# Graph layers on one core: where the inverse of the distance root is made for the third layer's first three units

## The chip, the cores and the metric

The kernel runs on one core of one Trainium2 chip. The metric is the device time of one execution in microseconds (us). The five instruction queues that matter here are PE (TensorE, the matmuls, with its weight loads shown apart as PEld), DVE (VectorE), ACT (ScalarE), POOL (GpSimd) and SP (SyncE, which issues loads). Each works through its own list in order and waits on semaphores that the others raise.

## The reference, cut to what matters

Four graph layers work on 4096 nodes of 64 features, x (4096 x 64), with one adjacency matrix adj (4096 x 4096). Each layer takes the layer norm of x, clips it below at zero, and adds its own result to x. The third (`L2_gnn`) is a layer in hyperbolic space. Cut to its core it is

```python
h = jnp.maximum(_layernorm(x, axis=-1), 0.0)          # 4096 x 64
deg = jnp.maximum(adj.sum(axis=1, keepdims=True), 1e-08)
w = adj / deg
log_ij = _logmap(h[:, None, :], h[None, :, :], c)      # c = 1, all pairs of nodes
agg = jnp.einsum('ij,ijc->ic', w, log_ij)
x = x + _expmap(0, agg @ weight + bias, c)

def _logmap(x, y, c):
    sub = _mobius_add(-x, y, c)
    sub_norm = norm(sub)
    arg = jnp.clip(sub_norm, 0.0, TANH_CLIP)
    return 2.0 / lam_x * jnp.arctanh(arg) * sub / sub_norm
```

For each pair of nodes the kernel needs one scalar out of this, arctanh(norm)/norm up to factors of the nodes. It gets it from a number z of the pair (a product of node rows): the root r = sqrt(z^2 - 1), the logarithm tau = ln(z + r), and the factor tau / r. The pair factor times the adjacency entry is then the weight with which a node's row enters the sum.

## The kernel before, in words

**Layers and units.** Layers run one after the other. The third layer walks the 4096 x 4096 square of pairs in 72 units (`UNITS`, lines 67 to 71), numbered n = 0 to 71. A unit is 256 nodes by 512, held as one tile of 128 partitions x 1024 columns (128x1024, f32). The pair factor is symmetric, so most units also serve the mirrored block: PE transposes them, and a second product with the adjacency entries (far) follows. Units 0 and 1 are not mirrored; unit 2 is the first that is. Units 0 to 2 are all full tiles.

**The work of one unit n**, by engine, with lines of the kernel before:
- PE `scores2(n)`: z of the unit into two PSUM banks of four matmuls (L859) and some small bf16 ones (L582). From n = 2 on it waits for `sum_ready` n - 1, the sum of unit n - 2, since there are two z buffers (`ROT` = 2).
- ACT `square2(n)`: z squared (L1243), raises `square_ready`.
- PE `sides2(n)`: small bf16 matmuls into the same banks (L582), raises `side_ready`.
- DVE `rest2(n)`: z^2 - 1, floored (L1977), raises `rest_ready`.
- ACT `roots2(n)`: the logarithm of that (L1249) into `lnr`; the exponential of half of it, which is the root, into `sums(n)` (L1257), raises `root_ready`; the exponential of minus half of it, which is the root's inverse, over the logarithm in `lnr` (L1260), raises `rin_ready`.
- DVE `sum2(n)`: waits for `root_ready` and `side_ready`, adds z and the root in place (L1983), raises `sum_ready`.
- ACT `arc2(n)`: the logarithm of the sum (L1264), raises `tau_ready`.
- DVE `pair2(n)`: waits for `tau_ready` and `rin_ready`, the product of the two (L1989), raises `pair_ready`.
- POOL: pair factor times adjacency (L560, near). PE `mirror2(n)`: eight transposes (L891), and DVE `far2(n)` multiplies them by the adjacency (L1996). Then PE gathers both (L582).

**Order.** The order on every engine is written out by hand. ACT runs, for each n: `roots2(n)`, extra steps, `square2(n + 1)`, `arc2(n)` (for n = 0 the square of unit 1 stands inside `roots2(0)`). DVE runs, for each n: copies of finished strips, `sum2(n)`, `far2(n - 1)` if mirrored, `rest2(n + 1)`, extra steps (`second_half2`, `last_passage2`), `pair2(n)`. PE runs, for each n: `scores2(n + 1)`, `sides2(n)`, `mirror2(n - 1)`, the gathers of unit n - 2. The extra steps are what is left of the second layer for its second half of the nodes, and pieces of the fourth: on DVE a copy of 128x1024 at n = 0 and at n = 2 (L1469, `second_half2`), and from n = 3 on rows of small operations.

**Buffers.** `lnr` and `root` have two slots, `sums` three. `roots2(n)` waits for `pair_ready` n - 1, the pair of unit n - 2, before it writes `lnr`. Loads of the adjacency for the units go through five slots that come free with the gathers.

Of the kernel before, what the change touches and what calls it, by code (L numbers as in the profile page):

```python
# [17 lines left out]
ACT = mybir.ActivationFunctionType  # L18
# [34 lines left out]
ROT = 2  # L53
# [18 lines left out]
HALVED = (4, 5, 6, 7)  # L72
FLIPS = (16, 18)
AUX_R, AUX_L = 13, 14


GROUPS = ((0, 8), (8, 16), (16, 32))
# [29 lines left out]
def mirrored(n):  # L107
    S, p = UNITS[n]
    return p >= 2 * S + 2 or S in HALVED and p == 2 * S
# [8 lines left out]
def first_col(n):  # L118

    S, p = UNITS[n]  # L120
    return PAIR if S in HALVED and p == 2 * S + 1 else 0


def mirrors(n):

    return sum(mirrored(m) for m in range(n + 1))
# [24 lines left out]
def graph_layers(nc, x, adj_t, codes, w0_t, b0, w1_t, b1, wq_t, bq, wk_t, bk, scalars, w2, b2, w3, b3, out):  # L151
    ctx = ExitStack()
    with ctx:
# [5 lines left out]
        def sem(name):  # L159
            if name not in named:  # L160
                named[name] = ctx.enter_context(nc.semaphore(name))
            return named[name]
# [78 lines left out]
        def units_of(first, n):  # L241
            return work[:, first * UNIT:(first + n) * UNIT].rearrange("p (k n) -> p k n", k=n)
        root, lnr = units_of(0, ROT), units_of(2, ROT)

        def sums(n):
            k = (4, 16, 17)[n % ROTS]
            return work[:, k * UNIT:(k + 1) * UNIT]
# [27 lines left out]
        def z_banks(n):  # L275
            return banks(4 + 2 * (n % ROT), 6 + 2 * (n % ROT))

        def live(ap, n):

            c = first_col(n)  # L280
            return ap.rearrange("p (q n) -> p q n", q=2)[:, :, c:] if c else ap
# [782 lines left out]
        def _(act):  # L1064
# [176 lines left out]
            def square2(n):  # L1241
                act.wait_ge(sem("z_ready"), n + 1)
                nc.scalar.activation(live(root[:, n % ROT, :], n), live(z_banks(n), n), ACT.Square).then_inc(sem("square_ready"), 1)  # L1243

            def roots2(n):
                act.wait_ge(sem("rest_ready"), n + 1)
                if n >= ROT:
                    act.wait_ge(sem("pair_ready"), n - ROT + 1)
                nc.scalar.activation(live(lnr[:, n % ROT, :], n), live(root[:, n % ROT, :], n), ACT.Ln).then_inc(sem("lnr_ready"), 1)  # L1249
                act.wait_ge(sem("lnr_ready"), n + 1)  # L1250
                if 0 < n < ROTS:
                    act.wait_ge(sem("agg1_done"), 4 * T - 2 + n)
                if n >= ROTS:
                    act.wait_ge(sem("near_ready"), n - ROTS + 1)
                    if mirrored(n - ROTS):
                        act.wait_ge(sem("mirror_ready"), mirrors(n - ROTS))
                nc.scalar.activation(live(sums(n), n), live(lnr[:, n % ROT, :], n), ACT.Exp, scale=0.5).then_inc(sem("root_ready"), 1)  # L1257
                if n == 0:
                    square2(1)
                nc.scalar.activation(live(lnr[:, n % ROT, :], n), live(lnr[:, n % ROT, :], n), ACT.Exp, scale=-0.5).then_inc(sem("rin_ready"), 1)  # L1260

            def arc2(n):
                act.wait_ge(sem("sum_ready"), n + 1)
# [70 lines left out]
            for n in range(NU):  # L1334
                roots2(n)
                last_passage2(n)
                second_half2(n)
                if 1 < n + 1 < NU:
                    square2(n + 1)
                arc2(n)  # L1340
# [56 lines left out]
        def _(dve):  # L1397
            V = nc.vector
# [580 lines left out]

            def sum2(n):  # L1980
                dve.wait_ge(sem("root_ready"), n + 1)
                dve.wait_ge(sem("side_ready"), n + 1)
                V.scalar_tensor_tensor(live(sums(n), n), live(z_banks(n), n), 1.0, live(sums(n), n), ALU.max, ALU.add)\  # L1983
                 .then_inc(sem("sum_ready"), 1)
# [36 lines left out]
            for n in range(NU):  # L2021
                if n >= 3 and mirrored(n - 3):
                    far2_out(n - 3)
                if n >= 3 and closes(n - 3) and n - 3 not in EARLY:
                    near2_out(n - 3)
                sum2(n)
                if n >= 1 and mirrored(n - 1):
                    far2(n - 1)
                if n + 1 < NU:
                    rest2(n + 1)  # L2030
                second_half2(n)
                last_passage2(n)
                if n - 2 in EARLY:
                    near2_out(n - 2)
                if n == NU - 1:
                    power(0)
                pair2(n)

            n = NU - 1
# [96 lines left out]
```

## Time and profile before

| what | value |
|---|---|
| median of 3 runs | 1099.08 us (1094.03 to 1100.4) |
| the profiled execution's own time | 1094.24 us |
| its span, from first instruction to last | 1092.5 us |
| busy share PE / DVE / ACT / POOL | 95% / 79% / 70% / 25% |
| mean granted TensorE clock | 0.989 |
| third layer's units | from 553.5 us to about 980 us |

The profile shows one execution. Busy time is the time in which an engine had an instruction in work; on an engine, the next instruction may start some 0.1 us before the one ahead of it ends. The chain of waits goes back from the last instruction to what released it, and "issue" in it is time for which the profile names no cause. A row of the timeline gives the start, the duration, and in brackets how long the engine sat idle before it and for whom.

### The profile page before, as it was taken

To read this page: it belongs to the slowest core of one execution; us is meant where nothing else is said; L and a number is where in the kernel's file an instruction comes from. 1 tells how busy PE (TensorE), PEld (TensorE's weight loads), DVE (VectorE), ACT (ScalarE), POOL (GpSimd) and SP (SyncE) were. 2 spreads that over 40 slices of the span, in tenths; PEclk is the share of its full clock that TensorE was granted. 3 is DMA by queue.
4 is the path that set the end of the run, shared out by engine and by line. 5 is a ranking of instruction groups with operands and counts; after the bars stand their busy time and mean duration, and the time that the engine had idled before them with its cause. 6 is when DMAs were issued, how large, how long until landed. Compare 5 with 4: busy or idle time off the path is not lost.

```text
span 1092.5 us, 14983 instructions
## 1 busy us (share of the span) xinstructions
PE 1035.0 (95%) x5462; PEld 451.6 (41%) x5462; DVE 859.5 (79%) x1021; ACT 760.0 (70%) x807; POOL 267.9 (25%) x146
## 2 busy tenths in 40 slices
PE   7999999999689999999979988999999998989998
PEld 2333333337633333334324443444544554436544
DVE  7999989996766666697669977887789887887781
ACT  4555455553556666686698989988888888886682
POOL 1089400000010000004015364434433433330010
PEclk9999999999989999999999999999999999999999
DMA  9999989980048888787754345555555546446441
GB/s 347 398 349 424 384 317 357 357 324 28 1 158 272 286 284 282 252 276 270 250 174 154 118 133 174 186 165 188 163 171 168 186 142 193 148 154 214 141 174 39
DMA packets 98453, 240.42 MB, mean 220 GB/s; under 512 B 16464, under 2 KB 47184, under 8 KB 82000
## 3 DMA queue, kind: packets, MB, share of 16 engines
q1 hardware_dynamic: 89168, 222.72, 60.1%
q10 hardware_dynamic: 9216, 16.78, 4.0%
q8 instruction: 43, 0.70, 0.2%
q14 instruction: 26, 0.21, 0.1%
HBM read 221.65 MB, written 17.83 MB: 219 GB/s over the span
## 4 chain that ended last, share of the span: by engine, by line
PE 53%; issue 21%; POOL 13%; DVE 7%; ACT 4%; DMA 1%; POOLq 0%; SPq 0%; DVEq 0%; ACTq 0%
PE PS L582 38%; POOL ring L560 10%; PE PS L756 5%; PE PS L757 5%; POOL H L560 2%; PE PS L594 1%; ACT work L1180 1%; DVE work L1989 1%; PE PS L616 1%; DMA X<-in_x 1%; PE PS L891 1%; DVE work L1621 1%; DVE ring L1996 0%; PE PS L907 0%; ACT work L1387 0%
## 5 line engine op out<-in xcount | busy, mean ns | idle before, releaser
L1662 DVE TENSOR_TENSOR work<-work,ring 128x1024 f32<-128x1024 f32 x128 | 151.2, 1223 | 76.6 <-ACT work L1180 76.5
L1180 ACT ACTIVATE work<-PS,att_sc 128x1024 f32<-128x1024 f32 x128 | 147.6, 1201 | 85.7 <-PE PS L757 78.4
L1115 ACT ACTIVATE work<-PS 128x1024 uint8<-128x1024 f32 x128 | 124.0, 1020 | 107.6 <-PE PS L582 107.6
L560 POOL TENSOR_TENSOR ring<-work,ring 128x1024 f32<-128x1024 f32 (+1 forms) x57 | 134.1, 2354 | 243.2 <-DVE work L1989 243.1
L582 PE MATMUL PS<-ring,work 128*65 128x256 f32 (+1 forms) x612 | 191.2, 460 | 2.4 <-DVE work L2017 1.5
L582 PE MATMUL PS<-work 128*64 128x512 f32 (+3 forms) x800 | 153.4, 523 | 1.1 <-ACT work L1243 1.0
L1983 DVE SCALAR_TENSOR_TENSOR work<-PS,work 128x1024 f32<-128x1024 f32 x72 | 85.9, 1193 | 55.0 <-PE PS L582 47.7
L582 PEld LDWEIGHTS PS<-ring,work 128*65 128x65 f32 x612 | 82.4, 138 | 89.7 <-issue 64.7
L756 PE MATMUL PS<-work 128*128 128x512 f16 x256 | 98.9, 386 | 2.0 <-DVE work L1469 1.3
L1249 ACT ACTIVATE work<-work 128x1024 f32<-128x1024 f32 x72 | 74.3, 1031 | 36.3 <-DVE work L1977 36.3
L757 PE MATMUL PS<-work 128*128 128x512 f16 x256 | 98.1, 383 | 0.0
L1989 DVE SCALAR_TENSOR_TENSOR work<-work 128x1024 f32<-128x1024 f32 x72 | 85.7, 1190 | 2.4 <-ACT work L1264 2.0
L582 PEld LDWEIGHTS PS<-work 128*64 128x64 f32 (+2 forms) x800 | 38.2, 119 | 118.5 <-issue 110.9
L1264 ACT ACTIVATE work<-work 128x1024 f32<-128x1024 f32 x72 | 74.2, 1030 | 12.4 <-DVE work L1983 10.2
L859 PE MATMUL PS<-TB,TA 64*128 64x512 f32 (+1 forms) x288 | 79.6, 629 | 2.9 <-DVE work L1983 2.9
L891 PE MATMUL PS<-ident,work 128*128 128x128 f32 x464 | 64.6, 282 | 18.3 <-DVE work L1989 17.1
L582 PE MATMUL PS<-work,TB 128*64 128x512 bf16 x672 | 76.4, 384 | 2.1 <-DVE work L1972 2.1
L1257 ACT ACTIVATE work<-work 128x1024 f32<-128x1024 f32 x72 | 74.4, 1033 | 2.3
L582 PE MATMUL PS<-work,tri_above 128*128 128x512 bf16 x256 | 75.8, 379 | 0.0
L1243 ACT ACTIVATE work<-PS 128x1024 f32<-128x1024 f32 x72 | 70.9, 985 | 5.2 <-PE PS L582 5.1
L582 PE MATMUL PS<-work,tri_rest 128*128 128x512 bf16 x248 | 74.4, 382 | 0.0
L1525 DVE TENSOR_TENSOR TB<-TB,work 128x2048 f32<-128x2048 f32 x32 | 73.4, 2293 | 0.1
(267 smaller groups left out, 1482.9 us busy)
## 6 DMA issues: line engine op xcount, KB each, us to landing
ring<-in_adj_t SPq DMA_DIRECT2D x96, 1024.0 KB, 5.7
ring<-in_adj_t SPq DMA_DIRECT2D x107, 512.0 KB, 4.0
work<-in_adj_t SPq DMA_DIRECT2D x32, 1024.0 KB, 8.4
codes<-work ACTq DMA_DIRECT2D x64, 256.0 KB, 7.3
ring<-codes SPq DMA_DIRECT2D x64, 256.0 KB, 4.0
H<-in_adj_t SPq DMA_DIRECT2D x25, 512.0 KB, 4.2
X<-in_x SPq DMA_DIRECT2D x2, 256.0 KB, 4.8
X<-in_x SPq DMA_DIRECT2D x1, 512.0 KB, 10.1
```

Of the source, the lines that this page charges most:

```text
L560: nc.gpsimd.tensor_tensor(live(near(n), n), live(sums(n), n), live(near(n), n), ALU.mult).then_inc(sem("near_ready"), 1)
L582: return mm(out_ap, lhsT, rhs, start=starts, stop=True, skip_group_check=True)
L756: mm(o, k_hl[:, jt * P:(jt + 1) * P], q_hh[:, i0:i0 + BANK], start=True, stop=False)
L757: ins = mm(o, k_hl[:, jt * P:(jt + 1) * P], q_ll[:, i0:i0 + BANK], start=False, stop=True)
L859: mm(z_banks(n)[:, q * BANK + c:(q + 1) * BANK], TA[half_rows(q), p * P:(p + 1) * P], TB[half_rows(q), S * STRIP + c:(S + 1) * STRIP], sta ...
L891: ins = nc.tensor.transpose(PS[:, c:c + P], sums(n)[:, q * BANK + i * P:q * BANK + (i + 1) * P], ident[:, :])
L1115: nc.scalar.activation(made[:, k, u * UNIT:(u + 1) * UNIT], PS[:, (4 + 2 * u) * BANK:(6 + 2 * u) * BANK], ACT.Relu).then_inc(sem("codes_ma ...
L1180: nc.scalar.activation(att[:, u, :], PS[:, (4 + 2 * u) * BANK:(6 + 2 * u) * BANK], ACT.Sigmoid, bias=att_sc[:, 2:3], scale=att_sc[:, 1:2]) ...
L1257: nc.scalar.activation(live(sums(n), n), live(lnr[:, n % ROT, :], n), ACT.Exp, scale=0.5).then_inc(sem("root_ready"), 1)
L1662: V.tensor_tensor(prob[:, m % 4, :], att[:, u, :], ring[:, s % RING, u * UNIT:(u + 1) * UNIT], ALU.mult)\
L1983: V.scalar_tensor_tensor(live(sums(n), n), live(z_banks(n), n), 1.0, live(sums(n), n), ALU.max, ALU.add)\
L1989: V.scalar_tensor_tensor(live(sums(n), n), live(sums(n), n), TAU_MAX, live(lnr[:, n % ROT, :], n), ALU.min, ALU.mult)\
```

## The change

For units 0, 1 and 2 of the third layer ACT no longer makes the inverse of the root. DVE makes it from the finished root, with its reciprocal instruction on the whole 128x1024 tile, as the first instruction of `sum2(n)`: behind the wait for `root_ready` and ahead of the sum that `scores2(n + 2)` and `arc2(n)` wait for. It writes the same `lnr` slot and raises the same `rin_ready`. Units 3 to 71 are as before.

```diff
+INVERTED = (0, 1, 2)
...
                 if n == 0:
                     square2(1)
-                nc.scalar.activation(live(lnr[:, n % ROT, :], n), live(lnr[:, n % ROT, :], n), ACT.Exp, scale=-0.5).then_inc(sem("rin_ready"), 1)
+                if n not in INVERTED:
+                    nc.scalar.activation(live(lnr[:, n % ROT, :], n), live(lnr[:, n % ROT, :], n), ACT.Exp, scale=-0.5)\
+                      .then_inc(sem("rin_ready"), 1)
...
             def sum2(n):
                 dve.wait_ge(sem("root_ready"), n + 1)
+                if n in INVERTED:
+                    V.reciprocal(lnr[:, n % ROT, :], sums(n)).then_inc(sem("rin_ready"), 1)
                 dve.wait_ge(sem("side_ready"), n + 1)
```

ACT, start of the third layer (L1243 square, L1249 logarithm, L1257 root, L1260 inverse of the root, L1264 logarithm of the sum), before:

```order
L1219 ACT_TABLE_LOAD
L1243 ACTIVATE work<-PS 128x1024
L1249 ACTIVATE work<-work 128x1024
L1257 ACTIVATE work<-work 128x1024
L1243 ACTIVATE work<-PS 128x1024
L1260 ACTIVATE work<-work 128x1024
L1264 ACTIVATE work<-work 128x1024
L1249 ACTIVATE work<-work 128x1024
L1257 ACTIVATE work<-work 128x1024
L1260 ACTIVATE work<-work 128x1024
L1243 ACTIVATE work<-PS 128x1024
```

The same place of ACT with the change (the lines move by two, and L1264 becomes L1268):

```order
L1221 ACT_TABLE_LOAD
L1245 ACTIVATE work<-PS 128x1024
L1251 ACTIVATE work<-work 128x1024
L1259 ACTIVATE work<-work 128x1024
L1245 ACTIVATE work<-PS 128x1024
L1268 ACTIVATE work<-work 128x1024
L1251 ACTIVATE work<-work 128x1024
L1259 ACTIVATE work<-work 128x1024
L1245 ACTIVATE work<-PS 128x1024
L1268 ACTIVATE work<-work 128x1024
```

The inverse is gone between the square of the next unit and the logarithm of the sum. ACT has three instructions fewer in all.

DVE with the change, from unit 2's reciprocal to its pair and on to the first mirrored product (L1989 sum, L2002 far, L1981 rest, L1473 a copy of the second layer, L1995 pair):

```order
L1987 RECIPROCAL work<-work 128x1024
L1989 SCALAR_TENSOR_TENSOR work<-PS,work 128x1024
L1981 TENSOR_SCALAR work<-work 128x1024
L1473 COPY work<-PS 128x1024
L1995 SCALAR_TENSOR_TENSOR work<-work 128x1024
L1989 SCALAR_TENSOR_TENSOR work<-PS,work 128x1024
L2002 TENSOR_TENSOR ring<-PS,ring 128x1024
L1981 TENSOR_SCALAR work<-work 128x1024
```

The first row is new; the others stand in the order that they had. DVE has three instructions more in all, each at the head of its unit. PE, POOL and SP keep their lists.

## Rows read from the trace of the kernel before

**Rows 1.** The page's busy time by engine, whole span.

```profile
PE 1035.0 (95%) x5462; PEld 451.6 (41%) x5462; DVE 859.5 (79%) x1021; ACT 760.0 (70%) x807; POOL 267.9 (25%) x146
```

**Rows 2.** Busy time in stretches: microseconds and instructions of each engine.

```profile
552.00:700.00 148.00, 132.43 (x662) 60.19 (x658) 120.90 (x147) 134.00 (x140) 68.65 (x41) 0.98 0.49 155
700.00:900.00 200.00, 198.34 (x974) 99.89 (x973) 164.01 (x220) 170.68 (x181) 80.12 (x35) 1.00 0.55 171
```

**Rows 3.** Chain of waits, start of the third layer: start, duration, what.

```profile
558.37 0.94 ACT work L1260
...
562.29 0.95 ACT work L1260
...
571.68 1.23 DVE work L1989
572.90 0.04 issue
572.95 1.98 PE PS L891 x8
574.96 1.23 DVE ring L1996
```

**Rows 4.** Timeline of ACT, units 0 and 1.

```profile
556.40 1.06 ACT L1257 ACTIVATE work<-work 128x1024 f32<-128x1024 f32 x1
557.36 1.01 ACT L1243 ACTIVATE work<-PS 128x1024 f32<-128x1024 f32 x1
558.27 1.05 ACT L1260 ACTIVATE work<-work 128x1024 f32<-128x1024 f32 x1
559.21 1.05 ACT L1264 ACTIVATE work<-work 128x1024 f32<-128x1024 f32 x1
560.16 1.04 ACT L1249 ACTIVATE work<-work 128x1024 f32<-128x1024 f32 x1
561.24 1.06 ACT L1257 ACTIVATE work<-work 128x1024 f32<-128x1024 f32 x1
```

**Rows 5.** Timeline of DVE, units 0 to 3.

```profile
557.49 1.23 DVE L1983 SCALAR_TENSOR_TENSOR work<-PS,work 128x1024 f32<-128x1024 f32 x1 [2.21 <-ACT work L1257]
558.63 0.68 DVE L1977 TENSOR_SCALAR work<-work 128x1024 f32<-128x1024 f32 x1
559.23 1.22 DVE L1469 COPY TA<-PS 128x1024 f32<-128x1024 f32 x1
560.36 1.22 DVE L1989 SCALAR_TENSOR_TENSOR work<-work 128x1024 f32<-128x1024 f32 x1
562.33 1.22 DVE L1983 SCALAR_TENSOR_TENSOR work<-PS,work 128x1024 f32<-128x1024 f32 x1 [0.75 <-ACT work L1257]
...
572.91 1.22 DVE L1983 SCALAR_TENSOR_TENSOR work<-PS,work 128x1024 f32<-128x1024 f32 x1
```

**Rows 6.** DVE's reciprocals by shape: count, busy us, mean ns of one, idle before.

```profile
L1716 DVE RECIPROCAL st<-st 128x16 f32<-128x16 f32 x2 | 0.5, 252 | 0.1
L1865 DVE RECIPROCAL st<-st 128x8 f32<-128x8 f32 x2 | 0.4, 202 | 0.1
...
L1810 DVE RECIPROCAL agg_y<-deg 128x32 f32<-128x32 f32 x1 | 0.3, 345 | 0.0
...
L1631 DVE RECIPROCAL att_sc<-scal 128x1 f32<-128x1 f32 x1 | 0.2, 155 | 0.0
```

**Rows 7.** Wide DVE operations, one line each: ns min/median/max, first and last start.

```profile
L1977 DVE TENSOR_SCALAR work<-work x72: 412/683/1480, 554.6 to 973.2; 128x1024 f32<-128x1024 f32 x68, 128x512 f32<-128x512 f32 x4
...
L1662 DVE TENSOR_TENSOR work<-work,ring x128: 1215/1220/1236, 308.6 to 552.3; 128x1024 f32<-128x1024 f32 x128
```

**Rows 8.** Timeline of PE, around unit 2's mirror.

```profile
568.45 1.13 PE L859 MATMUL PS<-TB,TA 64*128 64x512 f32 x4 [1.52 <-DVE work L1983]
569.51 0.84 PE L582 MATMUL PS<-work 9*128 9x512 bf16 x4
572.95 1.97 PE L891 MATMUL PS<-ident,work 128*128 128x128 f32 x8 [2.60 <-DVE work L1989]
...
579.72 1.09 PE L891 MATMUL PS<-ident,work 128*128 128x128 f32 x8 [0.48 <-DVE work L1989]
```

**Rows 9.** Busy time as in Rows 2; the third number from the end is the granted clock.

```profile
566.00:568.00 2.00, 0.92 (x3) 0.04 (x1) 1.19 (x2) 1.97 (x4) 1.57 (x1) 1.00 0.06 6
...
572.00:574.00 2.00, 1.05 (x5) 1.05 (x6) 1.98 (x2) 2.00 (x3) 1.03 (x1) 0.50 0.00 0
574.00:576.00 2.00, 2.00 (x7) 1.18 (x6) 1.18 (x2) 1.68 (x2) 1.34 (x1) 0.50 0.00 0
...
578.00:580.00 2.00, 1.52 (x11) 0.46 (x10) 1.93 (x5) 2.00 (x3) 0.26 (x1) 1.00 0.45 109
```

## The prediction, made before the changed kernel was run

> **What bounds the kernel now.** I read the busy time of the whole span first: PE is busy for 95% of it, DVE for 79% [rows 1]. That would say that work added to DVE is free. It is an average over stages, so the second view is the busy time in stretches. From 700 to 900 us, deep in the third layer, PE is busy for 198.3 of 200 us. At the layer's start, from 552 to 700 us, it is busy for only 132.4 of 148 us, and ACT for 134.0 [rows 2]. The start is thus not PE's. The third view, the chain of waits, says whose it is: in units 0 to 2 it runs through ACT, the inverse of the root (L1260) included, then over DVE's pair of unit 2 (L1989, to 572.9 us), PE's transposes of it (L891) and DVE's far product (L1996) [rows 3]. The timelines of ACT and DVE say how: ACT has five operations of 1.0 to 1.06 us in a unit, back to back [rows 4], while DVE idles 2.21 us ahead of unit 0's sum and 0.75 us ahead of unit 1's, both times for the root (L1257) [rows 5]. The sums of units 0, 1 and 3 start at 557.49, 562.33 and 572.91 us [rows 5].
>
> Two things follow. No later stage has stored work that could cover a late start: every list is in order, z has two buffers, and PE cannot make unit n + 2's z before unit n's sum. And once PE is full, a delay of the first units moves all that follows. So the question is how much later unit 2's pair and unit 3's sum come.
>
> **What the change removes.** Three exponentials of 1.05 us on ACT. They are on the chain now (two of them with 0.94 and 0.95 us [rows 3]), so this is worth something, but it is not all gained: the sum of each unit moves behind a DVE operation.
>
> **What it adds: the price of one reciprocal of 128x1024.** No such row exists before. Its nearest rows are reciprocals of 1, 8, 16 and 32 columns: 155, 202, 252 and 345 ns [rows 6]. From 1 to 32 columns that is (345 - 155) / 31 = 6.13 ns a column. A plain two-input operation of 1024 columns takes 1220 ns, that is, at most 1.19 ns a column [rows 7]. So the reciprocal is slow by the column, not by its start. With 6.13 ns, 1024 columns take 0.155 + 1023 x 0.00613 = 6.43 us; I take R = 6.4 us. The ends near this: the last stretch, 16 to 32 columns, has 5.8 ns a column, which gives 0.345 + 992 x 0.0058 = 6.1 us; 8 to 16 columns has 6.3, which gives 6.6 us. The far ends: 0.68 us, the fastest wide DVE operation here (L1977's median [rows 7]), and 8.7 us, if each column took eight of a plain operation's steps: (1220 - 155) / 1024 = 1.04 ns, and 0.155 + 1024 x 8 x 1.04 ns = 8.7 us.
>
> The page "VectorE: DVE Perf Modes" of the Trainium skill (section "First, the fixed hardware budget") says that the reciprocal is an iterative divide in the pipe with a repeat count of 8. By that rule R would be that far end, 8.7 us. Rows 6 speak against it, since eight steps would put 133 ns between 16 and 32 columns and the rows have 93; it is a rival below.
>
> **Where the reciprocals lie.** The reciprocal heads `sum2(n)`. Behind it in DVE's list wait the sum, the rest of unit n + 1, the copy (n = 0 and 2) and the pair; and for the sum wait ACT's logarithm and PE's z of unit n + 2. It covers nothing and nothing covers it: between the root and the sum DVE has no other work. I replay the units with durations from the rows. From the start of a reciprocal to the start of the next:
> - the reciprocal, R; then the sum, 1.23, which may start 0.09 us before the end of what is ahead of it (557.49 + 1.23 against 558.63 [rows 5]): R + 1.14;
> - ACT's logarithm of the sum starts 0.03 us later; the next unit's logarithm 0.95 us after that, its root 1.08 us later, and that ends after 1.06 us (559.21, 560.16, 561.24 and its duration [rows 4]); DVE starts 0.03 us after that: 3.15 us together.
>
> The rest of the next unit (0.68) is done when ACT needs it. In unit 0 the rest, the copy and the pair follow the sum and end at 557.49 + 6.4 + 4.1 = 568.0 us, just ahead of unit 1's root. A unit's step is R + 4.3 = 10.7 us, where it was 4.84 us. Unit 0's reciprocal starts where the sum did, 557.49; unit 1's at 568.2; unit 2's at 578.9 us. The pair of unit 2 follows its reciprocal, the sum (1.14), the rest (0.60 to the next start), the copy (1.13 to the next start) and its own 1.22 (the spacing of 557.49, 558.63, 559.23 and 560.36 [rows 5]): 578.9 + 6.4 + 4.1 = 589.4 us. Before, it ended at 572.9 [rows 3]. Delay: **16.5 us**, or 3R - 2.7 in general. Unit 3's sum comes at 578.9 + 10.7 = 589.6, where it was 572.91: 16.7, the same within the replay's grain.
>
> **PE's clock.** Before, the granted clock fell from 1.00 to 0.50 (from 2.4 to 1.2 GHz) after a stretch in which PE was busy for 0.92 of 2 us, stood at 0.50 from 572 to 576, and was back at 578 to 580 us. Unit 2's transposes took 1.97 us there against 1.09 us [rows 8, 9]. With the change PE has one small batch each 10.7 us until about 586 us, so it will be at 0.50 again, and earlier. Most of this is in the time before already. What is new: the z of unit 4 and the side terms of unit 3 (1.9 us from 568.45 on at full clock [rows 8]) start when unit 2's sum ends, near 586.4, and at half clock take 3.8 us, to 590.2. The transposes stand behind them: 0.8 us after the pair. I add it: 16.5 + 0.8 = 17.3 us. If the clock is up again, it is 16.5.
>
> **No cost, and why.** POOL's three products follow the pairs; POOL idles more, not less. The loads of units 5 and later wait for gathers that move by less than the units that use them. ACT saves 3 x 1.05 us in a stretch where it now waits for DVE's sum anyway: worth nothing beyond what the replay counts.
>
> **Sum.** The profiled execution took 1094.24 us (span 1092.5, and 1.7 around it); with 17.3 it takes 1111.5. The median of the three runs is 4.8 us above that execution; on it the sum is 1116.4. Two of the three runs lie at the upper value, so I take 1116.
>
> **Rivals.**
> - *The divide takes eight steps a column* (R = 8.7). Then 3 x 8.7 - 2.7 + 0.8 = 24.2 us, and 1123.3. For it: only the far extrapolation from 32 to 1024 columns. Against it: the spacing in rows 6. Chance 0.10.
> - *Not slower: the rate seen on short rows is a start-up cost, and a wide reciprocal streams* like the other single-input operation, in 0.68 us. Then 3 x 0.68 - 2.7 = -0.7 us, 1098.4. It holds within 1% of now (11 us) as long as R is below (11 + 2.7 - 0.8) / 3 = 4.3 us, that is 4 ns a column. Against it: 8, 16 and 32 columns lie on one line at about 6 ns. Chance 0.05.
> - *The delay is taken up later.* PE idles 15.6 us between 552 and 700 us [rows 2]; if half of those 17.3 us went into that idle time, 1107 or so would remain. Against it: the idle time comes of the same in-order waits that move along, and what PE does between is behind them. Chance 0.07, half of it within 1%.
> - *The exponential is not gone, or the reciprocal is narrower.* The order of instructions excludes it: three fewer on ACT, three more on DVE, all 128x1024. No chance.
>
> **Range and chances.** The forecast has 0.78: from 3 x 6.1 - 2.7 = 15.6 on the lower base (1109.8) to 3 x 6.6 - 2.7 + 0.8 = 17.9 on the highest run, 1100.4 (1118.3). To hold 8 in 10 with the unknown rate, the range takes in most of the eight-step rival: 1109 to 1123. A difference of 1% is about what a measurement of this kernel can tell. Slower by more than that: 0.91; within: 0.08; faster: 0.01, for which no row speaks.
>
> **What the changed profile would show.** Three reciprocals of 128x1024 near 6.4 us each, starting some 10.7 us apart from 557.5 us on, with no idle DVE time between the root and them; ACT idle for some 6 us ahead of each L1268 of units 0 to 2, with DVE's sum as releaser; unit 3's sum near 589.6 us; PEclk at half from about 565 to 593 us; and from there the same cadence, with the last unit and the end as much later as unit 3. Wrong would be: R off the line (each 0.1 us of R is 0.3 us); a shift at unit 3 that shrinks towards 700 us; or a step that is not R + 4.3.

## The result

The changed kernel took 1116.12 us (median of 4 runs, 1115.08 to 1118.69), the kernel before 1098.01 us beside it (4 runs, 1094.03 to 1100.4). The ratio is 1.0174, with a 95% interval from 1.0156 to 1.0192: slower by 18.1 us, by the interval 17 to 21 us. 1116 had been forecast, in a range from 1109 to 1123.

The profiled execution of the changed kernel took 1115.98 us, its span is 1114.3 us. That is 21.8 us more than the profiled execution of before, and the two do not begin the third layer at the same time. The section on `empty` below takes that apart.

### The profile page after: what moved, and what is told of

Its sections match the earlier page's. It is cut to its first block, busy times and chain, and to the rows that moved or that the text cites. A ratio compares the mean times of both kernels' runs of the same rounds, so it can differ in the third digit from the quotient of the medians.

```text
span 1114.3 us, 14980 instructions
## 1 busy us (share of the span) xinstructions
PE 1046.4 (94%) x5462; PEld 456.9 (41%) x5462; DVE 879.1 (79%) x1024; ACT 757.6 (68%) x804; POOL 241.0 (22%) x146
## 4 chain that ended last, share of the span: by engine, by line
PE 53%; issue 21%; POOL 13%; DVE 9%; ACT 3%; DMA 1%; POOLq 0%; SPq 0%; DVEq 0%; ACTq 0%
PE PS L584 38%; POOL ring L562 10%; PE PS L758 5%; PE PS L759 5%; POOL H L562 2%; DVE work L1987 2%; PE PS L596 1%; ACT work L1182 1%; DVE work L1995 1%; PE PS L618 1%; DMA X<-in_x 1%; PE PS L893 1%; PE PS L608 1%; DVE work L1981 0%; DVE ring L2002 0%
## 5 line engine op out<-in xcount | busy, mean ns | idle before, releaser
L584 PE MATMUL PS<-ring,work 128*65 128x256 f32 (+1 forms) x612 | 194.5, 467 | 2.4 <-DVE work L2023 1.5
L1989 DVE SCALAR_TENSOR_TENSOR work<-PS,work 128x1024 f32<-128x1024 f32 x72 | 85.7, 1190 | 51.5 <-PE PS L584 47.7
L861 PE MATMUL PS<-TB,TA 64*128 64x512 f32 (+1 forms) x288 | 82.5, 650 | 16.7 <-DVE work L1989 16.7
L1268 ACT ACTIVATE work<-work 128x1024 f32<-128x1024 f32 x72 | 74.2, 1030 | 31.7 <-DVE work L1989 29.6
L1995 DVE SCALAR_TENSOR_TENSOR work<-work 128x1024 f32<-128x1024 f32 x72 | 85.7, 1191 | 2.6 <-ACT work L1268 2.3
```

Source lines behind the costliest of these rows:

```text
L584: return mm(out_ap, lhsT, rhs, start=starts, stop=True, skip_group_check=True)
L861: mm(z_banks(n)[:, q * BANK + c:(q + 1) * BANK], TA[half_rows(q), p * P:(p + 1) * P], TB[half_rows(q), S * STRIP + c:(S + 1) * STRIP], sta ...
L1995: V.scalar_tensor_tensor(live(sums(n), n), live(sums(n), n), TAU_MAX, live(lnr[:, n % ROT, :], n), ALU.min, ALU.mult)\
```

## The profile after

First the page's busy time by engine, which answers to [rows 1]:

```profile
PE 1046.4 (94%) x5462; PEld 456.9 (41%) x5462; DVE 879.1 (79%) x1024; ACT 757.6 (68%) x804; POOL 241.0 (22%) x146
```

DVE has 19.6 us more in three instructions more, and its share of the span has not moved from 79%: the span grew with it. From this row alone the cost would not be seen. The timeline of DVE, units 0 to 3, answers to [rows 5] (in brackets the idle time ahead and what ended it):

```profile
561.33 6.55 DVE L1987 RECIPROCAL work<-work 128x1024 f32<-128x1024 f32 x1 [2.21 <-ACT work L1259]
567.80 1.16 DVE L1989 SCALAR_TENSOR_TENSOR work<-PS,work 128x1024 f32<-128x1024 f32 x1
568.87 0.68 DVE L1981 TENSOR_SCALAR work<-work 128x1024 f32<-128x1024 f32 x1
569.47 1.22 DVE L1473 COPY TA<-PS 128x1024 f32<-128x1024 f32 x1
570.60 1.22 DVE L1995 SCALAR_TENSOR_TENSOR work<-work 128x1024 f32<-128x1024 f32 x1
572.12 6.55 DVE L1987 RECIPROCAL work<-work 128x1024 f32<-128x1024 f32 x1 [0.30 <-ACT work L1259]
...
582.91 6.55 DVE L1987 RECIPROCAL work<-work 128x1024 f32<-128x1024 f32 x1 [0.81 <-ACT work L1259]
...
592.18 1.22 DVE L1995 SCALAR_TENSOR_TENSOR work<-work 128x1024 f32<-128x1024 f32 x1
593.69 1.23 DVE L1989 SCALAR_TENSOR_TENSOR work<-PS,work 128x1024 f32<-128x1024 f32 x1 [0.29 <-ACT work L1259]
```

A reciprocal takes 6.55 us. They start at 561.33, 572.12 and 582.91, 10.79 us apart. The timeline of ACT answers to [rows 4]:

```profile
560.24 1.06 ACT L1259 ACTIVATE work<-work 128x1024 f32<-128x1024 f32 x1
561.20 1.00 ACT L1245 ACTIVATE work<-PS 128x1024 f32<-128x1024 f32 x1
568.99 1.06 ACT L1268 ACTIVATE work<-work 128x1024 f32<-128x1024 f32 x1 [6.79 <-DVE work L1989]
569.95 1.04 ACT L1251 ACTIVATE work<-work 128x1024 f32<-128x1024 f32 x1
571.03 1.06 ACT L1259 ACTIVATE work<-work 128x1024 f32<-128x1024 f32 x1
```

ACT, which had run its operations back to back, now stands 6.79 us for the sum, once in unit 0, again in unit 1, and 5.87 us in unit 2. The chain of waits from unit 0's root to the first mirrored product answers to [rows 3]:

```profile
561.33 6.55 DVE work L1987
567.88 1.09 DVE work L1989
568.99 0.62 ACT work L1268
...
571.03 1.06 ACT work L1259
572.12 6.55 DVE work L1987
...
593.45 1.98 PE PS L893 x8
595.46 1.23 DVE ring L2002
```

The reciprocals are on it whole; the exponential for the inverse has left it. PE around unit 2's mirror answers to [rows 8]:

```profile
590.59 2.08 PE L861 MATMUL PS<-TB,TA 64*128 64x512 f32 x4 [5.22 <-DVE work L1989]
592.60 0.61 PE L584 MATMUL PS<-work 9*128 9x512 bf16 x4
593.45 1.97 PE L893 MATMUL PS<-ident,work 128*128 128x128 f32 x8 [0.24 <-DVE work L1995]
```

PE was at half clock (0.50 from 588 to 598 us): z took 2.08 us for 1.13. But the small matmuls behind it took 0.61 us for 0.84, and PE idled 0.24 us ahead of the transposes. In the kernel before, two of the small ones had to wait for the square of their unit (L1243, 568.89 to 569.90 us); here it was long done. The transposes started 0.05 us after the pair's end, as before. Unit 3's sum starts 32.36 us after unit 0's reciprocal; 589.6 - 557.49 = 32.1 had been forecast.

**A measure free of where the layer starts.** In all runs below I take the stretch from ACT's first square of the third layer to the end of unit 2's pair. Before: from 553.53 to 572.90, **19.37 us**. With the change: from 557.37 to 593.40, **36.03 us**. The change costs 16.66 us there. The starts of all 72 pairs, set beside each other, show what becomes of it: against the layer's start each pair from unit 2 to unit 67 is 16.61 to 16.66 us later than before. Nothing is given back over 380 us, and nothing is added. At units 68 and 69 comes a step of 2.8 us, which is not of the change, as `empty` will show.

## The experiments

To tell chance from the change, two more profiles were taken: the changed kernel once more (1115.85 us, span 1114.1) and the kernel before once more (1094.26 us, span 1092.5).

> The changed kernel once more, for a second profile. The stretch from the first square of the third layer to the end of unit 2's pair should be 36.0 us again, and the shift against before constant after it. If the 3.8 us by which the third layer began later, and the 2.8 us at units 68 and 69 at half clock, are of the change, they return; if they are of one execution, they differ.

The stretch was 36.03 us again, the layer began at 557.28 us, and the step at units 68 and 69 was 2.8 us again.

> The kernel before once more, for a second profile: 19.4 us from the first square of the third layer to the end of unit 2's pair. If the start of the third layer and the last units vary by some us between executions of one program, they differ from the first profile here too.

It was not so: 19.38 us, the layer's start at 553.54 us, no step. Two profiles of each agreed to 0.1 us in places where they should have differed if chance made them. Whether the change could then be behind these two terms is what the experiments `empty` and `small`, below, were for.

**One unit** (`one_unit`):

```diff
-INVERTED = (0, 1, 2)
+INVERTED = (0,)
```

> Only unit 0's inverse is made by DVE. Measured from the start of ACT's first square of the third layer to the end of unit 2's pair: 19.37 us before, 36.03 us with three units. Theory (the reciprocal lies on the loop root, sum, logarithm, next root; nothing covers it): unit 0's step becomes 10.8 us instead of 4.84, the other two stay as before, 25.3 us. Rival (DVE's added busy time of 6.55 us is partly covered by its idle time of 2.2 and 0.75 us in this stretch): 22.5 to 23.5 us. After unit 2 the shift should stay constant in both.

Measured: 25.45 us (1107.26 us the one run, 1096.46 us beside it for before). The step from unit 0's reciprocal to unit 1's sum is 570.87 - 560.09 = 10.78 us. Before, from sum to sum, it was 562.33 - 557.49 = 4.84 us. The theory holds: the 2.21 us of idle time ahead of unit 0's sum cover nothing, because that idle time is a wait for the very root that the reciprocal reads. Still the step grew by 5.94 us and not by 6.55. Before, ACT's five operations were the bound, and the sum was done 0.49 us before ACT took it up (557.49 + 1.23 against 559.21, [rows 4, 5]); that slack goes first. The 0.15 us above the forecast is mostly one longer rest of unit 2 (0.91 us for 0.68). The whole execution is longer by more than that, because half-clock steps like the one at unit 68 stand in it too: 2.8 us between units 60 and 65, and 1.5 us at units 68 and 69.

**Half a tile** (`half`):

```diff
-                if n not in INVERTED:
-                    ... ACT.Exp, scale=-0.5 ...
+                part_ = slice(BANK, UNIT) if n in INVERTED else slice(0, UNIT)
+                own = lnr[:, n % ROT, part_]
+                ...
+                if n in INVERTED:
+                    act.wait_ge(sem("root_ready"), n + 1)
+                nc.scalar.activation(own, own, ACT.Exp, scale=-0.5).then_inc(sem("rin_ready"), 1)
...
-                    V.reciprocal(lnr[:, n % ROT, :], sums(n)).then_inc(sem("rin_ready"), 1)
+                    link(V.reciprocal(lnr[:, n % ROT, 0:BANK], sums(n)[:, 0:BANK]))
```

> DVE makes the inverse of columns 0 to 511 of units 0 to 2, ACT that of columns 512 to 1023. Theory (the price is by the column, about 6.25 ns): a reciprocal of 128x512 takes 3.35 us, the step of a unit 3.45 + 4.25 = 7.7 us, and the stretch from the first square to the end of unit 2's pair 26.7 us (36.03 with whole tiles, 19.37 before). ACT's half exponential of some 0.6 us is hidden behind the reciprocal. Rival (a good part of the 6.55 us is a cost of the wide instruction, its start or its buffers): over 4 us each, 29 us or more.

DVE's timeline of this kernel, unit 0:

```profile
559.87 3.35 DVE L1990 RECIPROCAL work<-work 128x512 f32<-128x512 f32 x1 [2.21 <-ACT work L1259]
563.26 1.23 DVE L1992 SCALAR_TENSOR_TENSOR work<-PS,work 128x1024 f32<-128x1024 f32 x1
```

3.35 us, and 26.98 us for the stretch against 26.7 forecast (1107.83 us the one run, 1096.46 us beside it for before). The price is by the column: (6.55 - 3.35) / 512 = 6.25 ns, on top of a start of 0.15 us.

**Both** (`both`):

```diff
-                if n not in INVERTED:
-                    ... ACT.Exp, scale=-0.5 ...
+                nc.scalar.activation(... lnr ..., ACT.Exp, scale=-0.5).then_inc(sem("rin_ready"), 1)
...
-                    V.reciprocal(lnr[:, n % ROT, :], sums(n)).then_inc(sem("rin_ready"), 1)
+                    V.reciprocal(root[:, n % ROT, :], sums(n))
```

> ACT keeps its exponential for the inverse in units 0 to 2, and DVE's reciprocals run as well, at the same places, into a buffer that is free (their result is not used). Theory (the removed exponentials are worth nothing, since ACT then waits 6 us for DVE's sum): 36.0 us from the first square to the end of unit 2's pair, as with the change. Rival (the removed exponentials give back 1.05 us each, so that the reciprocals cost more than the replay says): 39.2 us.

Measured: 36.03 us, and 1116.25 us in all (one run, 1096.46 us beside it for before). The three exponentials that the change removes are worth nothing: with or without them ACT stands and waits for the sum.

**Behind the sum** (`behind`):

```diff
             def sum2(n):
                 dve.wait_ge(sem("root_ready"), n + 1)
-                if n in INVERTED:
-                    V.reciprocal(...)
                 dve.wait_ge(sem("side_ready"), n + 1)
+                to = root[:, n % ROT, :] if n in INVERTED else sums(n)
...
                 if n + 1 < NU:
                     rest2(n + 1)
+                if n in INVERTED:
+                    link(V.reciprocal(lnr[:, n % ROT, :], sums(n)))
...
             def square2(n):
                 act.wait_ge(sem("z_ready"), n + 1)
+                if n - ROT in INVERTED:
+                    act.wait_ge(sem("pair_ready"), n - ROT + 1)
```

> Units 0 to 2: the sum goes to the free root slot, and DVE's reciprocal moves behind the sum and the next unit's rest, so that PE and ACT get the sum at once and only the pair waits for the reciprocal. Theory (DVE's own list becomes the bound: sum 1.14, rest 0.6, reciprocal 6.6, copy 1.13 in units 0 and 2, pair 1.13): steps of 10.6 and 9.5 us, 34.8 us from the first square to the end of unit 2's pair, 1.2 us less than the change. Rival (the position ahead of the sum is what costs, and behind it the reciprocal runs beside ACT's and PE's work): 20 to 26 us.

Measured: 37.26 us, 1.2 us more than the change and not 1.2 less. The whole execution took 1114.55 us (one run), less than the changed kernel's 1115.98, but its third layer had begun at 552.99 us and not at 557.37, so that is no gain of this order. The rival is out by far: having the sum early does not help when the pair, and with it DVE's list, waits 6.55 us. My step was too short. DVE's timeline of this kernel, unit 1:

```profile
566.41 1.21 DVE L1999 SCALAR_TENSOR_TENSOR work<-work 128x1024 f32<-128x1024 f32 x1
567.55 1.22 DVE L1991 SCALAR_TENSOR_TENSOR work<-PS,work 128x1024 f32<-128x1024 f32 x1
568.78 1.91 DVE L1984 TENSOR_SCALAR work<-work 128x1024 f32<-128x1024 f32 x1
570.60 6.54 DVE L2042 RECIPROCAL work<-work 128x1024 f32<-128x1024 f32 x1
577.18 1.23 DVE L1999 SCALAR_TENSOR_TENSOR work<-work 128x1024 f32<-128x1024 f32 x1
```

DVE has no idle time from one pair to the next. The rest (L1984) took 1.91 us where it takes 0.68: it fell beside POOL's product of the pair just made, which is this row:

```profile
567.77 2.36 POOL L562 TENSOR_TENSOR ring<-work,ring 128x1024 f32<-128x1024 f32 x1 [62.01 <-DVE work L1999]
```

The product ended at 570.13 and the rest at 570.69, 0.56 us later; for the next rest (579.55, 1.83 us) it was 0.54 us. That reads as a rest which is held until the product is done. The two took 1.91 and 1.83 us for 0.68, which is 2.4 us, nearly the whole distance between 34.8 and 37.26.

**Later units** (`later_units`):

```diff
-INVERTED = (0, 1, 2)
+INVERTED = (25, 28, 31)
```

> The three reciprocals stand in units 25, 28 and 31 instead of 0, 1 and 2, where PE is busy without a gap and DVE idles some 20%. Theory (the slack there is what a row shows: the sum may come 0.7 us and PE's mirror 1.5 us later before PE waits; the rest is lost): the pair of each comes 5.8 us late, PE stands 4.3 us, and all that follows is some 13 us later, 10 to 15. Rival (DVE has idle time there and PE two z buffers, so the reciprocals are covered): 0 to 4 us.

Measured: 1116.37 us (4 runs) against 1096.0, a ratio of 1.0183 (1.0166 to 1.0200), about 20 us. The shift of the pairs, each against its own layer's start, is 0 up to unit 24, 6.96 at unit 27, 13.62 at unit 30 and 20.28 from unit 33 on. Both theories missed; the rival most. PE of this kernel, unit 25's mirror:

```profile
710.62 1.13 PE L861 MATMUL PS<-TB,TA 64*128 64x512 f32 x4 [2.68 <-DVE work L1989]
711.68 0.40 PE L584 MATMUL PS<-work 9*128 9x512 bf16 x4
713.48 1.97 PE L893 MATMUL PS<-ident,work 128*128 128x128 f32 x8 [1.41 <-DVE work L1995]
715.25 5.52 PE L584 MATMUL PS<-H,work 128*65 128x512 f32 x12
720.70 1.13 PE L861 MATMUL PS<-TB,TA 64*128 64x512 f32 x4
```

and the same unit in the kernel before, whose third layer began 1.80 us sooner:

```profile
707.46 1.09 PE L891 MATMUL PS<-ident,work 128*128 128x128 f32 x8
708.39 3.61 PE L582 MATMUL PS<-H,work 128*65 128x512 f32 x12
711.93 1.13 PE L859 MATMUL PS<-TB,TA 64*128 64x512 f32 x4
```

The transposes are late by 713.48 - 1.80 - 707.46 = 4.2 us: the 4.3 us of the theory, which three times over would have been its 13 us. But after PE had stood for 2.68 and 1.41 us its clock was at half, and transposes and gathers ran to the next z in 7.22 us instead of 4.47. That is 2.75 us more, and 4.22 + 2.75 = 6.97 us for this reciprocal. The other two cost 6.66 us each, and eight transposes took 1.97 us behind each of them too. The clock was left out of the forecast. The rows of busy time (third number from the end is the granted clock) of this kernel:

```profile
700.00:705.00 5.00, 5.00 (x27) 2.58 (x26) 4.34 (x5) 3.22 (x4) 2.36 (x1) 1.00 0.51 141
705.00:710.00 5.00, 2.94 (x11) 1.24 (x9) 5.00 (x2) 0.00 (x0) 0.00 (x0) 1.00 0.52 172
710.00:715.00 5.00, 2.97 (x15) 1.92 (x16) 4.25 (x6) 3.70 (x4) 1.49 (x1) 0.73 0.51 175
715.00:720.00 5.00, 5.00 (x13) 2.02 (x12) 3.60 (x4) 4.75 (x6) 2.21 (x2) 0.59 0.00 0
720.00:725.00 5.00, 5.00 (x26) 2.31 (x25) 3.12 (x4) 2.67 (x3) 1.04 (x1) 1.00 0.62 190
```

So in all three places a stall of PE in a stretch where it is full cost its own length and then the half clock. In units 0 to 2 the clock's share is nearly nil, since the stretch before the change ran unit 2's mirror at half clock already [rows 8, 9].

**No unit, and three small ones** (`empty`, `small`). `empty` is the changed text with `INVERTED = ()`; `small` is `both` with 16 columns:

```diff
-                    V.reciprocal(root[:, n % ROT, :], sums(n))
+                    link(V.reciprocal(root[:, n % ROT, 0:16], sums(n)[:, 0:16]))
```

> The changed kernel's text with no unit inverted by DVE: every engine has the instructions of the kernel before, in the same order. The three kernels with whole reciprocals in units 0 to 2, in unit 0 and in later units began the third layer at 557.4, 556.1 and 555.3 us instead of 553.5, though nothing stands changed ahead of it, and each did so again in a second profile where one was taken. If that comes of the changed lists of instructions, this kernel is at 553.5 us, and 19.4 us from there to the end of unit 2's pair; if it comes of the text or its line numbers, it is elsewhere.

> ACT keeps its exponential, and DVE makes three reciprocals of 128x16 at the places of the whole ones (result not used). Theory (ACT's five operations are the bound of a unit before, and the sum may come up to 0.5 us later before the logarithm of the sum waits for it): a reciprocal of 0.25 us and its wait are free, 19.4 us from the first square to the end of unit 2's pair. Rival (anything between the root and the sum is on the path): 3 x 0.3 us more, 20.3 us. And if the third layer again begins later than 553.5 us, that is no work of the reciprocals, since these take no time worth naming.

`empty`: 1097.66 us (10 runs), ratio 1.0002 (0.9992 to 1.0012). `small`: 1098.33 us (10 runs), ratio 1.0013 (0.9999 to 1.0026). The stretch is 19.37 us in both. In `small` unit 0's pair came 0.29 us later and unit 1's no later at all. So a DVE operation of 0.25 us and its wait between root and sum is free: it fits into the 0.49 us by which the sum was early for ACT.

The profile of `empty` answers the other question. It has the instructions of the kernel before, in their order; still its third layer began at 557.41 us, not 553.5, and it shows the step at unit 68. The changed lists of instructions are thus not needed for either. `small` began its third layer later still, at 558.52 us, and has no step at unit 68; `both` began at 554.77 and `behind` at 552.99 us. ACT's first square and PE's transposes of unit 68 in `empty`:

```profile
557.41 1.02 ACT L1245 ACTIVATE work<-PS 128x1024 f32<-128x1024 f32 x1
...
964.97 1.97 PE L893 MATMUL PS<-ident,work 128*128 128x128 f32 x8 [2.94 <-DVE work L1995]
966.73 5.42 PE L584 MATMUL PS<-ring,work 128*65 128x512 f32 x12
```

The kernel before, at the same place:

```profile
961.09 1.09 PE L891 MATMUL PS<-ident,work 128*128 128x128 f32 x8 [2.94 <-DVE work L1989]
962.02 3.61 PE L582 MATMUL PS<-ring,work 128*65 128x512 f32 x12
```

The profiled span of `empty` is 1097.5 us; the changed kernel's is 1114.3. The difference is 16.8 us, and the stretch says 16.66.

The distance between `empty` and the kernel before, 1097.5 against 1092.5 us, lies in four places, and in each of them PE's instructions took up to twice their time in one of the two. The first two lie ahead of the third layer. PE in `empty`, at both:

```profile
12.05 3.68 PE L584 MATMUL PS<-ring,H 128*64 128x512 f32 x8 [1.91 <-DVE H L1503]
...
280.29 3.44 PE L608 MATMUL PS<-ident,work 128*128 128x128 f32 x16 [1.65 <-DVE work L1628]
```

PE in the kernel before, at both:

```profile
12.38 1.94 PE L582 MATMUL PS<-ring,H 128*64 128x512 f32 x8 [2.27 <-DVE H L1499]
...
277.78 1.09 PE L606 MATMUL PS<-ident,work 128*128 128x128 f32 x8 [1.66 <-DVE work L1624]
279.28 1.06 PE L606 MATMUL PS<-ident,work 128*128 128x128 f32 x8 [0.41 <-DVE deg L1574]
```

| place | `empty` late against before, up to here |
|---|---|
| first matmuls of the first layer, 12 to 20 us | 2.5 us |
| transposes of the second layer, 280 to 284 us | 3.9 us |
| unit 68 of the third layer | 6.5 us |
| fourth layer, 990 to 994 us, where it is the kernel before that is slow | 5.0 us |

The granted clock of `empty` reads 0.50 from 282 to 284 us, and that of before 0.56 and 0.59 from 990 to 994 us. At 12 to 18 us it reads 1.00 in `empty` and in the changed kernel, though the matmuls took twice as long; in `one_unit`, `both`, `half` and `later_units` it reads 0.50 or little more for a part of that stretch, so there the half clock is read from the durations. The changed kernel shows the same four: 2.6 and 1.2 us ahead of the third layer, 16.66 us for the change, 2.8 us at units 68 and 69, less the 1.6 us that only the kernel before loses in its fourth layer. That is 21.7 of the 21.8 us. Why the clock fell in one execution and not in the other stays open; the idle time ahead was 1.91 us in `empty` and 2.27 in before at the first place, 1.65 and 1.66 at the second.

## Why the prediction was right, point by point

- **What bounds the start.** Right. Before, it was ACT's five operations, 4.84 us a unit, with 0.49 us to spare for the sum; with the change it is the loop root, reciprocal, sum, logarithm, next root. The 21% that DVE idles over the span covered nothing. `one_unit`, `small` and the constant shift of 66 pairs show it.
- **R.** 6.4 us was taken, 6.55 measured; the range was 6.1 to 6.6. The rate from reciprocals of 1 to 32 columns, 6.13 ns a column, held to 2% at 1024 columns (6.25). That is six of the prediction's steps of 1.04 ns, an estimate from a plain operation. The rival of eight steps a column is out: 8.7 us against 6.55. It is the one that the rule of the Trainium skill ("VectorE: DVE Perf Modes", "First, the fixed hardware budget": a repeat count of 8) would have given, and there the measurement decides against it.
- **The step.** R + 4.3 was forecast, with R = 6.55 that is 10.85; measured 10.79, the difference in the sum's 1.16 us for 1.23.
- **The delay.** 3R - 2.7 with the measured R is 16.95 us; measured 16.66. The 0.3 us between are the two steps, 0.06 us each too long in the replay, and 0.16 us in unit 2's last part (593.40 - 582.91 = 10.49 for 10.65). In the sum of 17.3 a short R (0.45 us too little) and the clock's term (0.8 us too much) partly made up for each other; that 17.3 lies within 0.7 us of 16.66 is in part luck.
- **The clock's term failed.** 0.8 us was added for a PE at half clock that holds up unit 2's transposes; it was 0.0. I had doubled 1.9 us for z and side terms. z did double nearly (2.08 for 1.13), but the 0.84 us of small matmuls in the row of before contain a wait for a square, which was not there any more (such matmuls took 0.39 to 0.40 us elsewhere at full clock, and 0.61 here). The clock itself was not at half throughout, as had been forecast from 565 to 593 us: it reads 0.71 and 0.72 between 572 and 580 and 0.93 between 584 and 588 us.
- **The removed exponentials.** Forecast as worth nothing beyond the replay; `both` shows it.
- **Given back later.** A chance of 0.07 had been left for it. Not a tenth of a microsecond was given back up to unit 67.
- **The total.** 1116 had been forecast and 1116.12 came; that they meet so closely is luck. The forecast put 17.3 us on a base near 1099, the median of three runs; the four beside the changed kernel have 1098.01, and later ones 1096.0 (7 runs) and 1096.7 (19 runs). For the profiled execution 1111.5 us had been forecast and 1115.98 came: the half-clock places outside the stretch, which `empty` has too, are not of the change and were in no term.
- **What stays open.** The two profiled executions differ by 21.8 us, the medians by 18.1, the stretch by 16.66. The medians' interval begins at 17.1 us, somewhat above 16.7. Single executions of the kernel before lie between 1093.69 and 1100.4 us; whether the rest is that scatter or more half-clock places in the unprofiled executions with the change, these runs do not say.

No version here beats the kernel before: every placement of a reciprocal on DVE that was tried costs 2.5 to 7 us a unit at whole or half width, and the one that costs nothing is 16 columns wide.

## What to carry to other kernels

An instruction put between a producer and its first consumer costs its length, less the time by which the consumer was late anyway, when the engine's idle time there is a wait for that same producer. The engine's busy share says nothing of it. Here the consumer was late by 0.49 us: 0.25 us were free, and a single 6.55 us cost 6.1. Price an operation that the trace has only in small shapes by the slope between two sizes, not by its name, and count the columns: 6.25 ns a column for this divide against 1 ns on ACT. Compare two profiles from a common event inside the changed stage, here its first instruction, since the stages ahead of it differed by up to 5.5 us here (552.99 to 558.52 us) with the same instructions in them.

## What the hardware showed that was not expected

- PE had idled 2.94 us ahead of unit 68's transposes in the kernel before and in `empty`, for the same reason. The clock stayed up in one and was at half in the other: 1.09 against 1.97 us for eight transposes, 3.61 against 5.42 us for the gathers behind them. The idle time just ahead does not alone decide. Four such places make up the 5.0 us between these two executions.
- A single-input DVE operation on 128x1024 f32 (the rest) takes 0.68 us alone and up to 1.91 us beside POOL's product of the pair (128x1024, 2.36 us). Each longer one, here and in the kernel before (1.04, 1.43 and 1.48 us), ended 0.54 to 0.56 us after that product did, so it looks held and not slowed. It is not so for all: one rest beside another POOL operation of that shape (L523) took 0.68 us. DVE's sums and far products, which read one tensor from PSUM (PS), stayed at 1.21 to 1.23 us beside the product, and the reciprocal at 6.55.
- Profiles of the same program agreed to some 0.1 us at each pair; the profile of `empty`, which has the same list of instructions in another program, was 3.9 us behind at the start of the third layer. The kernel before and the changed kernel were profiled twice each and kept their own times, `empty` once, so whether it goes with the program's text or with the execution is open.
